# Two indirect scatters of ranks 2 and 3 in flight instead of one, in a mixture-of-experts layer on one core

## The chip, the core and the metric

The kernel runs on one core of a Trainium2 chip, in one launch. The metric is the device time of that launch in microseconds (us). Times of the profile are counted from the start of the span of one profiled execution.

## What is computed

```python
x = layernorm(x + diagonal_ssm_layer(x, Wd, bd, Wi, bi, gamma, beta))
gate = einsum('bsd,ed->bse', x, Wg) + routing_bias
_, top_idx = top_k(gate, 4)
weights = softmax over the 4 chosen, 0 elsewhere
out = swiglu(x, Ws1, Ws2, Ws3)
eo = swiglu of x with each expert's W1, W2, W3
out = out + einsum('ebsd,bse->bsd', eo, weights)
x = layernorm(x + out)
```

There are 2 x 2048 = 4096 tokens of width 256, 8 experts with a hidden size of 682, and 4 experts for each token. The shared expert (Ws1 to Ws3) sees every token. The first layer is a scan along the sequence; it and the routing come before the part that the change touches.

## The kernel before

**Data.** `y_rows` holds the 4096 normed tokens in SBUF as 32 tiles of 128 rows; a row has the token's high and low half-precision parts and its 8 expert weights (264 words of 4 bytes, so a tile is 135 KB). `rows_by_place` (`xs` in the code) is a table in DRAM in which each expert has a contiguous run of places, padded to whole groups of 128 rows. A token stands in it 4 times, once for each of its experts. Its places are sorted, so rank 0 is the place with the token's lowest expert and rank 3 that with its highest.

**Scatter.** On POOL (GpSimd), `scatter(k, overlapped, beside)` (L628 to L641) issues 32 indirect DMAs (L637), one for each tile, that write the tile's rows to their places of rank k. The ranks come one after the other, 0, 1, 2, 3, and after each a `pad_rows` (L623) writes zeros into the padding places of an expert. Two semaphores, `scattered[k][0]` and `scattered[k][1]`, count the even and the odd tiles. For `n < overlapped` tile n waits only for tile n - 2, so two scatters can be in flight; else tile n waits for tile n - 1. Rank 0 has `overlapped` 20, the others have 0.

**Conversion.** The weights of an expert arrive as one DMA of 2.2 MB into the one buffer `stage` (`fetch`, L560), and 12 steps on POOL turn them into a high and a low half-precision part in one of two weight sets in `work` (L563, L564, L570, L573), after which `weight_set_ready` is raised. Expert e uses set e % 2, so its conversion can't start before TensorE (PE) has done with expert e - 2. POOL's program has them in this order:

- the steps of expert 1 between the scatters of rank 1;
- the steps of expert 2 between scatters 1 to 12 of rank 3, with a wait for the end of expert 0 ahead of them (`convert_beside`, L643);
- the fetch of expert 3's weights behind scatter 16 of rank 3;
- after rank 3 the zeros of experts 3 to 7, each of which waits for the one before;
- then a loop over e (L696 to L706). At e = 1 POOL waits for the end of expert 1 and converts expert 3 (`convert(4, 1)`; index 0 is the shared expert's), then fetches the next weights. At e = 2 it waits for the end of expert 2 and converts expert 4, and so on. From e = 4 on each turn also gathers one rank of the experts' results back into `y_sum` (`combine`, L688): 32 indirect DMAs (L682), after the rows of expert e are stored.

**TensorE.** PE runs 9 blocks of 256 tokens of the shared expert, then the experts' blocks by pairs of experts, then the other 7 shared blocks. A block is 66 matmuls up (L942) and 34 down (L965, L970); at the end of an expert there may be a half block of 128 tokens (`xb_half` in the names). Before an expert PE waits for its weight set (L1019). Even experts use the tiles `xb`, odd ones `xb_odd`.

**Loads.** SP loads a block's rows from `rows_by_place` by two transposing DMAs and one small one (`row_weights`), for block b once PE has done the up part of block b - 2. For expert e < 4 it waits first for all of rank e and for the zeros of expert e (L486 to L489).

Between up and down, ACT (L779, L785) and DVE (L1262, L1271) gate the block. L1271 subtracts the high part `g_hi` from `g`, both in SBUF.

Of the kernel before, what the change touches and what calls it, by code (L numbers as in the profile page):

```python
# [59 lines left out]
def build(nc, xT, x_tok, small, wpack, out):  # L60
# [8 lines left out]
    NT = N // P  # L69
# [41 lines left out]
    with ctx:  # L111
# [194 lines left out]
        def low_rank(s):  # L306

            return LOW_ORDER.index(s) + 1
# [9 lines left out]
        def counted(eng, sem_, value):  # L318

            eng.wait_ge(sem_, value)  # L320
            eng.sem_inc(passed, 1)
# [55 lines left out]
        def blocks_until(eng, e):  # L377

            full, half, first, _ = expert_row(eng, e)
            return eng.snap(eng.snap(first + full) + half)  # L380
# [115 lines left out]
        def _(pool):  # L496
# [61 lines left out]
            def fetch(n):  # L558

                pool.dma_start(stage[:, :], wpack[n]).then_inc(weights_loaded, 16)  # L560
# [28 lines left out]
            def convert_step(t, n, w, i):  # L589

                a, m = pieces[i // 2]
                if i == 0:
                    pool.wait_ge(weights_loaded, 16 * n + 16)
                if i % 2 == 0:
                    high_part(t, w, a, m)
                else:
                    t.wait()
                    low_part(t, w, a, m)
                if i == 2 * len(pieces) - 1:
                    t.wait()  # L600
                    pool.sem_inc(weight_set_ready, 1)

            def conversion(n):
                return Tally(pool, convert_steps, 3 * len(pieces) + 1, n - 2)
# [16 lines left out]
            def pad_rows(e):  # L621

                pool.indirect_dma_start(  # L623
                    out=xs, out_offset=bass.IndirectOffsetOnAxis(ap=pad_at[:, e:e + 1], axis=0),
                    in_=zeros[:, :], in_offset=None, bounds_check=NG * P - 1, oob_is_err=False)\
                    .then_inc(pads_written[e], 16)

            def scatter(k, overlapped=0, beside=None):  # L628

                for n in range(NT):  # L630
                    if k == 0 and n % JT == 0:
                        pool.wait_ge(y_low_ready, low_rank(B * (n % (NT // B) // JT) + n // (NT // B)))
                    if n > 1 and (n < overlapped or overlapped and n % 2 == 0):
                        pool.wait_ge(scattered[k][n % 2], 16 * (n // 2))
                    if n > 0 and (n >= overlapped and (n % 2 == 0 or not overlapped)):
                        pool.wait_ge(scattered[k][(n - 1) % 2], 16 * ((n - 1) // 2 + 1))
                    pool.indirect_dma_start(  # L637
                        out=xs, out_offset=bass.IndirectOffsetOnAxis(ap=place[:, k, n:n + 1], axis=0),
                        in_=y_rows[:, n, :], in_offset=None).then_inc(scattered[k][n % 2], 16)
                    if beside:  # L640
                        beside(n)  # L641

            def convert_beside(e, first, fetched):  # L643

                t = conversion(e + 1)

                def step(n):
                    if n == first and e >= 2:
                        counted(pool, down_ready, blocks_until(pool, e - 2) + S1)
                    if 0 <= n - first < 2 * len(pieces):  # L650
                        convert_step(t, e + 1, e % 2, n - first)
                    if n == fetched:
                        fetch(e + 2)
                return step
# [8 lines left out]
            scatter(1, 0, convert_beside(1, 5, 20))  # L663
            pad_rows(1)
            pool.wait_ge(pads_written[1], 16)
            scatter(2)
            pad_rows(2)
            pool.wait_ge(pads_written[2], 16)
            scatter(3, 0, convert_beside(2, 1, 16))
            for e in range(3, E):  # L670
                pool.wait_ge(pads_written[e - 1], 16)
                pad_rows(e)
# [784 lines left out]
```

## Time and profile before

| | us |
|---|---|
| median of 3 runs | 1080.36 (1077.96 to 1081.9) |
| the profiled execution, its time | 1077.3 |
| its span | 1075.5 |
| PE busy (matmuls) | 1007.5 (94%) |
| DVE busy | 581.8 (54%) |
| POOL busy | 533.4 (50%) |
| ACT busy | 501.6 (47%) |
| mean granted TensorE clock | 0.982 of full speed |

Busy shares are means over very different stages; a busy PE is not a PE at its peak, since matmuls are pipelined. POOL's issuing of an indirect DMA counts as busy time, the wait for its landing doesn't. A wait is put down to what the profile infers from semaphore events; "issue" is idle time that it can't put down to anything.

### The profile page before, as it was taken

How to read it: one execution, taken by the hardware profiler on the slowest of the kernel's cores; microseconds unless marked ns; L12 is line 12 of the kernel's file. 1: busy time of each engine (PE TensorE's matmuls, PEld its weight loads, DVE VectorE, ACT ScalarE, POOL GpSimd, SP SyncE). 2: the span in 40 equal slices, each digit the busy share in tenths (PEclk: the TensorE clock that was granted, in tenths of full speed). 3: DMA queues.
4: the chain of work that ended last, by engine and by line, in shares of the span. 5: the costliest groups of instructions: out<-in, count | busy, mean ns of one | idle time of the engine just before them, and what ended most of it. 6: DMA issues, size and time to landing. Idle time of an engine off the chain costs nothing.

```text
span 1075.5 us, 27303 instructions
## 1 busy us (share of the span) xinstructions
PE 1007.5 (94%) x8784; PEld 856.1 (80%) x8785; DVE 581.8 (54%) x1598; ACT 501.6 (47%) x1282; POOL 533.4 (50%) x486
## 2 busy tenths in 40 slices
PE   7997989999999999999889999999999999999985
PEld 3556878778888888888678878978888888888874
DVE  3998896455343435534543435454454444344677
ACT  3675553344454444445334534444444544454454
POOL 3554064376233338623761025075778773676761
PEclk9998999999999999999889999999999999999998
DMA  7846133532633333352234124118763664766674
GB/s 231 225 112 159 21 91 91 153 87 85 168 95 96 86 105 89 94 164 85 56 108 128 49 50 123 44 45 174 113 104 62 110 105 76 119 99 100 86 140 107
DMA packets 167876, 113.84 MB, mean 106 GB/s; under 512 B 113420, under 2 KB 160015, under 8 KB 166672
## 3 DMA queue, kind: packets, MB, share of 16 engines
q0 software_dynamic: 30480, 59.41, 25.7%
q1 hardware_dynamic: 115088, 32.33, 14.9%
q10 hardware_dynamic: 22256, 21.50, 5.8%
q8 instruction: 21, 0.34, 0.2%
q14 instruction: 31, 0.25, 0.1%
HBM read 47.09 MB, written 40.96 MB: 82 GB/s over the span
## 4 chain that ended last, share of the span: by engine, by line
PE 39%; DMA 33%; issue 10%; POOL 9%; DVE 5%; ACT 1%; SPq 1%; ACTq 0%; POOLq 0%; DVEq 0%
PE psA L942 25%; DMA rows_by_place<-y_rows,place 23%; PE psB L965 9%; DMA y_sum<-rows_by_place,place 6%; POOL rows_by_place L637 3%; POOL work L570 2%; PE psA L893 2%; DMA rows_by_place<-zeros,pad_at 2%; PE psB L970 1%; POOL stage L564 1%; POOL work L563 1%; PE psC L924 1%; SPq L475 1%; DMA xb<-rows_by_place 1%; DVE work L1070 1%
## 5 line engine op out<-in xcount | busy, mean ns | idle before, releaser
L1262 DVE SCALAR_TENSOR_TENSOR g<-psA,sil 128x256 f32<-128x256 f32 (+1 forms) x510 | 207.9, 414 | 439.6 <-ACT sil L779 432.5
L779 ACT ACTIVATE sil<-psA 128x256 f32<-128x256 f32 (+1 forms) x510 | 187.2, 373 | 301.7 <-PE psA L942 253.7
L682 POOL DMA_INDIRECT y_sum<-rows_by_place,place x128 | 200.3, 1565 | 105.8 <-DMA y_sum<-rows_by_place,place 78.4
L942 PE MATMUL psA<-xb_odd,work 128*128 128x256 f16 x2112 | 238.4, 274 | 9.0 <-issue 6.0
L637 POOL DMA_INDIRECT rows_by_place<-y_rows,place x128 | 130.3, 1018 | 220.6 <-DMA rows_by_place<-y_rows,place 173.6
L942 PE MATMUL psA<-xb,work 128*128 128x256 f16 x2046 | 231.9, 275 | 7.8 <-DMA row_weights<-rows_by_place 3.8
L942 PEld LDWEIGHTS psA<-xb_odd,work 128*128 128x128 f16 x2112 | 206.9, 98 | 36.7 <-issue 11.4
L785 ACT ACTIVATE g_hi<-g 128x256 f16<-128x256 f32 (+1 forms) x510 | 206.3, 405 | 56.6 <-DVE g L1262 50.9
L965 PE MATMUL psB<-work,g_hi 128*128 128x256 f16 x1320 | 222.1, 273 | 8.1 <-DVE g_lo L1271 7.6
L942 PEld LDWEIGHTS psA<-xb,work 128*128 128x128 f16 x2046 | 201.1, 99 | 34.6 <-issue 9.8
L1271 DVE TENSOR_TENSOR g_lo<-g,g_hi 128x256 f16<-128x256 f32 (+1 forms) x425 | 207.2, 488 | 10.5 <-ACT g_hi L785 6.7
L965 PE MATMUL psB<-work,g_lo 128*128 128x256 f16 x660 | 180.2, 273 | 0.0
L965 PEld LDWEIGHTS psB<-work,g_hi 128*128 128x128 f16 x1320 | 126.3, 98 | 30.1 <-DVE g_lo L1271 14.6
L942 PE MATMUL psA<-xb,wshared 128*128 128x256 f16 x1056 | 120.3, 274 | 3.8 <-DVE g L1262 2.6
L942 PEld LDWEIGHTS psA<-xb,wshared 128*128 128x128 f16 x1056 | 103.4, 98 | 18.0 <-DVE g L1262 3.9
L563 POOL TENSOR_SCALAR work<-stage 128x704 f16<-128x704 f32 (+1 forms) x42 | 37.2, 886 | 122.9 <-PE psB L970 113.3
L965 PEld LDWEIGHTS psB<-work,g_lo 128*128 128x128 f16 x660 | 64.7, 98 | 7.6
L893 PE MATMUL psA<-work,sm 128*128 128x512 f32 x128 | 59.0, 610 | 6.1 <-DMA work<-xT 6.1
L570 POOL TENSOR_TENSOR work<-stage,work 128x704 f16<-128x704 f32 (+2 forms) x42 | 63.1, 1503 | 2.9
L965 PE MATMUL psB<-wshared,g_hi 128*128 128x256 f16 x320 | 54.3, 273 | 8.8 <-DVE g_lo L1271 8.4
L811 ACT ACTIVATE eb<-psB,row_weights_odd 128x256 f32<-128x256 f32 x64 | 26.9, 471 | 70.1 <-PE psB L970 56.6
L811 ACT ACTIVATE eb<-psB,row_weights 128x256 f32<-128x256 f32 x62 | 26.0, 471 | 70.1 <-PE psB L970 53.8
(137 smaller groups left out, 708.2 us busy)
## 6 DMA issues: line engine op xcount, KB each, us to landing
stage<-wpack POOLq DMA_DIRECT2D x9, 2176.0 KB, 9.0
rows_by_place<-eb ACTq DMA_DIRECT2D x63, 256.0 KB
work<-xT SPq DMA_DIRECT2D x8, 512.0 KB, 4.7
work<-half_beta SPq DMA_DIRECT2D x8, 512.0 KB, 5.0
work<-x_tok POOLq DMA_DIRECT2D x8, 512.0 KB, 6.0
rows_by_place<-y_rows,place POOLq DMA_INDIRECT x128, 2.5
y_sum<-rows_by_place,place POOLq DMA_INDIRECT x128, 4.0
out<-y_sum ACTq DMA_DIRECT2D x4, 512.0 KB, 3.7
```

Of the source, the lines that this page charges most:

```text
L563: t.add(pool.tensor_scalar(parts_of(w, a, m)[0], stage[:, a:a + m], WS, 1.0, ALU.mult, ALU.mult))
L570: t.add(pool.tensor_tensor(lo[:, 0:full], stage[:, a:a + full], hi[:, 0:full], ALU.subtract))
L637: pool.indirect_dma_start(out=xs, out_offset=bass.IndirectOffsetOnAxis(ap=place[:, k, n:n + 1], axis=0), in_=y_rows[:, n, :], in_offset=No ...
L682: pool.indirect_dma_start(out=y_sum[:, n, :], out_offset=None, in_=xs, in_offset=bass.IndirectOffsetOnAxis(ap=place[:, k, n:n + 1], axis=0 ...
L779: act.activation(sil[r0:r0 + n, c % SLOTS, 0:T], psA[0:n, c % HVS, 0:T], ACT.Silu, scale=1.0 / (XS * WS)).then_inc(silu_ready, 1)
L785: act.activation(g_hi[0:n, c, 0:T], g32[0:n, c % SLOTS, 0:T], ACT.Copy).then_inc(gated_high_ready, 1)
L811: last = act.activation(eb[:, j, :], psB[:, j, 0:D], ACT.Copy, scale=row_weights[slot][:, j, e:e + 1])
L893: last = pe.matmul(psA[:, q, :], wdi[:, m, w, k, :], xt[b][:, k, :], start=(k == 0), stop=(k == KD - 1))
L942: last = pe.matmul(dst, W[:, ws, k, ci, :], xb[slot][:, KD * xs_ + k, 0:T], start=(k == 0 and n == 0), stop=(k == KD - 1 and n == 2))
L965: pe.matmul(o, a[:, c, j * P:(j + 1) * P], W3[:, ws, c, :], start=(c == 0 and n == 0), stop=False)
L1262: dve.scalar_tensor_tensor(g32[0:n, c % SLOTS, 0:T], src, 1.0 / (XS * WS), sil[r0:r0 + n, c % SLOTS, 0:T], ALU.mult, ALU.mult).then_inc(ga ...
L1271: dve.tensor_tensor(dst, g32[0:n, c % SLOTS, 0:T], g_hi[0:n, c, 0:T], ALU.subtract)\
```

## The change

`scatter` is called with `overlapped` = NT = 32 for ranks 2 and 3 in place of 0. Every tile n > 1 of these ranks then waits for tile n - 2 and not for tile n - 1. Nothing is added or moved on any engine: the instructions and their order are the same on all five, only POOL's waits differ.

```diff
@@ -663,10 +663,10 @@
             scatter(1, 0, convert_beside(1, 5, 20))
             pad_rows(1)
             pool.wait_ge(pads_written[1], 16)
-            scatter(2)
+            scatter(2, NT)
             pad_rows(2)
             pool.wait_ge(pads_written[2], 16)
-            scatter(3, 0, convert_beside(2, 1, 16))
+            scatter(3, NT, convert_beside(2, 1, 16))
             for e in range(3, E):
                 pool.wait_ge(pads_written[e - 1], 16)
                 pad_rows(e)
```

The zeros behind rank 2 (L623) wait for no scatter, before and now, and the first scatter of rank 3 waits for these zeros, not for rank 2's last tile.

## Rows read from the trace of the kernel before

**Rows 1.** Page, part 4: the chain that ended last, by line.

```profile
PE psA L942 25%; DMA rows_by_place<-y_rows,place 23%; PE psB L965 9%; DMA y_sum<-rows_by_place,place 6%; POOL rows_by_place L637 3%; POOL work L570 2%; PE psA L893 2%; DMA rows_by_place<-zeros,pad_at 2%; PE psB L970 1%; POOL stage L564 1%; 
```

**Rows 2.** Timeline of PE: start us, us, engine, line, names, count, idle before.

```profile
524.88 4.14 PE L942 MATMUL psA<-xb_half,work 128*128 128x128 f16 x66 [0.22 <-issue]
...
534.35 0.61 PE L970 MATMUL psB<-work,g_hi 106*128 106x256 f16 x2
540.71 0.61 PE L942 MATMUL psA<-xb_odd,work 128*128 128x256 f16 x2 [5.75 <-issue]
...
554.49 1.04 PE L942 MATMUL psA<-xb_odd,work 128*128 128x256 f16 x8
...
566.82 0.94 PE L942 MATMUL psA<-xb_odd,work 128*128 128x256 f16 x7 [0.46 <-DMA xb_odd<-rows_by_place]
```

**Rows 3.** Windows: us, PE, PEld, DVE, ACT, POOL busy, clock, DMA share, GB/s.

```profile
524.80:540.70 15.90, 7.78 (x83) 5.04 (x83) 6.53 (x12) 4.25 (x15) 14.86 (x15) 0.74 0.17 43
...
345.00:404.00 59.00, 58.94 (x540) 52.76 (x541) 25.02 (x63) 27.37 (x74) 19.67 (x20) 1.00 0.34 96
```

**Rows 4.** Timeline of POOL, from rank 3's scatter 13 to expert 3's conversion.

```profile
444.43 1.24 POOL L637 DMA_INDIRECT rows_by_place<-y_rows,place  x1 [0.82 <-POOL work L573]
...
504.48 1.00 POOL L623 DMA_INDIRECT rows_by_place<-zeros,pad_at  x1 [0.31 <-issue]
...
519.24 0.77 POOL L563 TENSOR_SCALAR work<-stage 128x704 f16<-128x704 f32 x1 [0.93 <-issue]
...
538.78 0.66 POOL L573 TENSOR_TENSOR work<-stage,work 64x256 f16<-64x256 f32 x1
```

**Rows 5.** Line 637 in 308 to 404 us, then in 136 to 170 us.

```profile
L637 POOL DMA_INDIRECT rows_by_place<-y_rows,place x32: 969/969/1212, 308.6 to 400.0; - x32
```

```profile
L637 POOL DMA_INDIRECT rows_by_place<-y_rows,place x20: 965/972/1953, 136.3 to 169.3; - x20
```

**Rows 6.** Timeline of PE: the end of expert 1 and expert 2's first block.

```profile
478.46 0.60 PE L970 MATMUL psB<-work,g_hi 106*128 106x256 f16 x4
480.67 1.59 PE L942 MATMUL psA<-xb,work 128*128 128x256 f16 x13 [1.61 <-DMA row_weights<-rows_by_place]
```

**Rows 7.** Timeline of PE: starts of blocks at other changes of expert.

```profile
641.09 1.29 PE L942 MATMUL psA<-xb,work 128*128 128x256 f16 x7 [2.02 <-issue]
...
653.94 1.04 PE L942 MATMUL psA<-xb,work 128*128 128x256 f16 x8
...
697.63 1.06 PE L942 MATMUL psA<-xb_half,work 128*128 128x128 f16 x16
...
705.71 1.04 PE L942 MATMUL psA<-xb_odd,work 128*128 128x256 f16 x8 [0.88 <-DMA xb_odd<-rows_by_place]
...
717.39 1.16 PE L942 MATMUL psA<-xb_odd,work 128*128 128x256 f16 x9
```

**Rows 8.** Timeline of PE: two blocks of the shared expert during rank 0.

```profile
164.86 1.37 PE L942 MATMUL psA<-xb,wshared 128*128 128x256 f16 x11
...
175.78 1.48 PE L942 MATMUL psA<-xb,wshared 128*128 128x256 f16 x12
```

**Rows 9.** Lines by form, DVE: 345 to 404 us, then 639 to 660 us.

```profile
L1271 DVE TENSOR_TENSOR g_lo<-g,g_hi 128x256 f16<-128x256 f32 x26 | 10.9, 421 | 0.7 <-ACT g_hi L785 0.3
```

```profile
L1271 DVE TENSOR_TENSOR g_lo<-g,g_hi 128x256 f16<-128x256 f32 x7 | 5.9, 837 | 0.0
```

**Rows 10.** Timeline of POOL: first gathers of ranks 2 and 3.

```profile
907.34 1.54 POOL L682 DMA_INDIRECT y_sum<-rows_by_place,place  x1 [14.32 <-DMA rows_by_place<-eb]
...
981.12 1.54 POOL L682 DMA_INDIRECT y_sum<-rows_by_place,place  x1 [3.76 <-DMA rows_by_place<-eb]
```

**Rows 11.** Timeline of SP: one block's load; then PE: that block's start.

```profile
352.92 2.72 SPq L475 DMA_TRANSPOSE xb_odd<-rows_by_place  x2
357.50 0.39 SPq L481 DMA_DIRECT2D row_weights_odd<-rows_by_place  x1
```

```profile
366.91 1.26 PE L942 MATMUL psA<-xb_odd,work 128*128 128x256 f16 x10
```

## The prediction

> **What bounds the kernel now.** I read four views. The chain of waits first: its largest entries are PE's up matmuls and the landings of the scatters of L637, 23% [rows 1]. That share misleads. A chain is followed back through whatever released each step, and for 370 us it runs down POOL's column while PE is busy beside it, all of 58.94 of 59 us between 345 and 404 [rows 3]. A scatter costs the end something only where POOL is late for somebody, so the second view is PE's timeline, to see where PE stood still. There is one large hole: PE ends expert 2 at 534.35 + 0.61 = 534.96 and starts expert 3 at 540.71, idle for 5.75 us with no releaser named [rows 2]. The third view, POOL's timeline, names it: the last instruction of expert 3's conversion starts at 538.78 and takes 0.66, so the weights are ready at 539.4 [rows 4]. The conversion began at 519.24, though PE had done with expert 1, which frees the set, at 478.46 + 0.60 = 479.06 [rows 6]. For 40.2 us POOL had been busy with rank 3 and the zeros. So here POOL's queue, by way of the weight set, is the bound, and nowhere else before the tail. The fourth view, the windows, adds that PE's granted clock is 0.74 around the hole [rows 3], between its two levels of 1.2 and 2.4 GHz, after 1.00 in the steady stretch.
>
> **How early POOL becomes.** Rank 2 issues 32 scatters from 308.6 to 400.0, so 91.4 / 31 = 2.95 us each. Rank 0's first 20, with two in flight, go from 136.3 to 169.3, so 33.0 / 19 = 1.74 us each [rows 5]. I take 1.74; the bounds are 2.95 (a pair gains nothing) and 1.27 (0.97 of issue and the 0.30 that stands between two issues). Rank 2 gains 31 x 1.21 = 37.5 us. In rank 3 the scatters between conversion steps gain nothing: there POOL's arithmetic paces them. From scatter 13 at 444.43 to the first zeros behind rank 3 at 504.48 [rows 4] there are 18 plain intervals, which gain 18 x 1.21 = 21.8. The five zeros keep their waits, 14.8 us from 504.48 to 519.24. Together POOL is 59 us earlier and would reach the turn e = 1 at about 460. There it now waits for expert 1, until 479.1. So of 59 us 40 count, and 19 are slack: a pace up to (91.4 + 58.8 - 40.2) / 49 = 2.24 us would do as well, with 58.8 us from 444.43 to the start of rank 3's last scatter, 1.27 before 504.48.
>
> **What PE gets.** I count from expert 2's first block at 480.67 [rows 6] to expert 3's third at 566.82 [rows 2], 86.15 us before: four full blocks, a half block, two full blocks. Without hole or disturbance a full block takes 175.78 - 164.86 = 10.92 [rows 8]. From a half block to the first block of the next expert in the same pair it is 705.71 - 697.63 = 8.08 [rows 7], against 540.71 - 524.88 = 15.83 now [rows 2]. That makes 6 x 10.92 + 8.08 = 73.60, a gross gain of 12.55 us. It holds the hole, the half block that was slow beside the conversion and at the low clock, and the 2.86 and 1.41 us by which the two blocks at 540.71 and 554.49 exceed 10.92.
>
> **What is given back.** Expert 3's conversion doesn't vanish, it moves to 479.4, beside expert 2's first two blocks. And POOL then fetches expert 4's weights at about 500, so expert 4's conversion starts at once when expert 2 ends, near 532, beside expert 3's first blocks. A conversion slows DVE: L1271 takes 837 ns beside one and 421 ns without [rows 9]. What reaches PE is less, since DVE has idle time in a block. The nearest rows are two conversions that also start at an expert's end: the block at 641.09 takes 12.85, so 1.93 over, and that at 705.71 takes 11.68, so 0.76 over; no later block of either is slow [rows 7]. The first is at a change of pair, as 1 to 2 is; the second is within a pair after a half block, as 2 to 3 is. So I take 1.93 for expert 3's conversion and 0.76 for expert 4's. The upper bound for either is 2.86 + 1.41 = 4.27, the two blocks of expert 3 that now run beside expert 4's conversion [rows 2], which holds clock too; the lower is 0.76. Expert 2's conversion, between the scatters of rank 3, moves 39 us forward from one steady block to another at the same POOL pace: nothing. The fetch behind scatter 16 moves with it: nothing, since the row loads have room (below).
>
> By the Trainium skill's page "SBUF — State Buffer", section "Who interferes with whom", a DVE instruction with two SBUF inputs contends with a GpSimd instruction that reads SBUF, and the loser blocks for a whole instruction. L1271 and all conversion steps are such instructions; were each of L1271's six instructions of a block to wait out a 1.5 us step on PE's path, two blocks would lose 6 x 2 x 1.5 = 18 us, and the sum would be a loss. The trace shows 0.42 us more for each, and 0.76 to 1.93 for a block, so the price of the rows stands.
>
> **The sum.** 12.55 - 1.93 - 0.76 = 9.86 us, bounds 12.55 - 2 x 4.27 = 4.0 and 12.55 - 2 x 0.76 = 11.0. Does it reach the end? Downstream POOL starts each turn when an expert ends or its rows are stored: the gathers of rank 2 waited 14.32 us for expert 6's rows and those of rank 3 waited 3.76 us for expert 7's [rows 10]. These waits are on PE's progress, so POOL follows when PE is earlier, and the last gathers, which end the kernel, start 9.86 us earlier with everything behind them unchanged. The profiled execution would go from 1077.3 to 1067.4. The median stands 3.1 us above the profiled execution; I subtract from the median: 1080.36 - 9.86 = **1070.5 us**.
>
> **Rivals.**
>
> *No overlap in the queue.* The second scatter might only wait behind the first. Pace 2.95, POOL as late as before, 1080.4. Rank 0's pace speaks against it [rows 5], though rank 0 ran beside blocks whose input came from SBUF, not from the table. It decides where POOL gains under about 6 us of its possible 59, so at a pace above 2.83. Chance 0.07.
>
> *The gain is given back.* Both moved conversions cost 4.27 us as in [rows 2]: 12.55 - 8.54 = 4.0, so 1076.4. For it speaks that such a price was measured where expert 4's conversion ran; against it that part of that price was the clock after a hole that will be gone. Chance 0.09.
>
> *Slower: row loads held back.* With two scatters writing to DRAM the loads of expert rows land later. The place is SP's loads for the blocks beside plain scatters: 31 x 1.74 = 54 us of rank 2 and 18 x 1.74 = 31 us of rank 3, about 8 blocks. A load of which the last part is issued at 357.50 + 0.39 and lands some 2.5 us later, taking a scatter's landing for it, is there by 360.4, and its block starts at 366.91 [rows 11]. So 6.5 us are free, and only a load delayed by more than that costs anything. At 8.4 us of delay each block would lose 1.9, 15.2 in all, and the kernel would be slower by 15.2 - 9.86 = 5.3, so 1085.7. A second scatter adds one landing, 2.5 us, so I see no way there. The page "DMA: Bandwidth & Descriptors", section "Queues, rings and completion order", of the Trainium skill says that a semaphore's write lands only after every earlier write of its DMA engine, across its queues; by that rule a load's completion waits for the scatters' writes too, and if loads had no room, 8 blocks x 2.5 us would give 1090.5. The blocks beside rank 0 show no such delay, 10.92 us [rows 8], though their loads read SBUF. Chance 0.03.
>
> *Something downstream keeps part of it*, such as a conversion that falls on a worse moment or gathers that meet other traffic: 1075 to 1079. Chance 0.06.
>
> **How the numbers follow.** The forecast holds 0.75. A measurement of this kernel can tell about 0.5%, 5.4 us, from no change. Of the forecast's range, 4.0 to 11.0 us of gain, nearly all is beyond that. Faster: 0.75, and 0.04 from partial versions of the rivals that still gain over 5.4, so 0.79. Within 0.5%: the first two rivals and the last, 0.17 with what they cede. Slower: 0.04, the third rival and what is unforeseen. The range runs from 1067 (the best case 1069.4, and the 2.4 us by which the lowest of the three runs was under the median) to 1077 (the second rival's 1076.4).
>
> **What would show it.** In the changed profile: L637's 31 intervals of rank 2 take about 54 us; POOL waits for PE's down matmuls ahead of expert 3's conversion, some 19 us that weren't there; that conversion runs from 479.4 to 500; PE has no hole between experts 2 and 3, and 8.1 us stand between the starts of the half block and the next; the clock stays near 1.00 there; L1271 is near 800 ns in 480 to 500, and expert 2's first block takes some 12.8. I am wrong if the hole is there, if blocks beside the plain scatters take more than 10.92, or if the two conversions cost more than 4 us together.

## The result, and the profile after

The changed kernel takes **1113.22 us** (median of 4 runs, 1105.73 to 1117.57), the kernel before 1081.13 beside it (4 runs, 1077.96 to 1083.79): a ratio of 1.0291, interval 1.0225 to 1.0357. I had forecast 1070.5 with 1077 as the upper end. It is slower, where I had given that 4 in 100.

The profiled execution took 1115.4 us, its span is 1113.6, 38.1 more than the 1075.5 before. The page: totals, two rows of the 40 slices, the chain's first lines.

```profile
PE 1023.0 (92%) x8784; PEld 858.2 (77%) x8785; DVE 578.1 (52%) x1598; ACT 502.1 (45%) x1282; POOL 533.3 (48%) x486
...
PE   7997999899975888999999999999999999999985
...
PEclk9998999899995889999999999999999999999998
...
PE 69%; DVE 11%; issue 7%; DMA 5%; ACT 4%; SPq 2%; POOL 1%; ACTq 1%; DVEq 0%; another core or an unknown queue 0%; POOLq 0%
```

DVE, ACT and POOL have the same busy time as before within 4 us. Slices 12 and 13, some 306 to 362 us, have a PE of 7 and 5, and in the second the clock is at 5: that is where rank 2 is scattered. In the chain the scatters have gone from 23% [rows 1] to the 2% that the page gives L637's landings now, and "issue" is at 7%. The windows cut the stretch up:

```profile
core 0: us, PE busy (x) PEld busy (x) DVE busy (x) ACT busy (x) POOL busy (x), PEclk, DMA share, GB/s
312.00:324.00 12.00, 12.00 (x112) 10.75 (x111) 4.22 (x11) 4.62 (x12) 7.15 (x9) 1.00 0.38 113
324.00:337.00 13.00, 5.84 (x32) 3.40 (x31) 2.79 (x7) 2.59 (x7) 9.44 (x10) 0.74 0.34 114
337.00:349.00 12.00, 8.80 (x34) 3.87 (x34) 0.00 (x0) 0.46 (x2) 8.50 (x10) 0.50 0.27 98
349.00:362.00 13.00, 3.78 (x12) 0.94 (x10) 0.26 (x1) 0.77 (x3) 8.36 (x9) 0.50 0.33 116
```

PE goes from 112 matmuls in 12 us to 32 in 13, 34 in 12 and 12 in 13. Its clock falls to 0.50, the lower level of 1.2 GHz, within the 13 us of which it stands still for more than half. The DMA engines are hardly busier than they were: share 0.27 to 0.38 and 98 to 116 GB/s, against 0.34 and 96 in the steady stretch before [rows 3]. Inside the up part of one block, PE, PE's weight loads and POOL run so:

```profile
352.02 0.10 PEld L942 LDWEIGHTS psA<-xb,work 128*128 128x128 f16 x1 [1.31 <-issue]
352.71 0.37 PE L942 MATMUL psA<-xb,work 128*128 128x256 f16 x1 [1.02 <-issue]
352.92 0.97 POOL L637 DMA_INDIRECT rows_by_place<-y_rows,place  x1 [0.63 <-issue]
353.41 0.10 PEld L942 LDWEIGHTS psA<-xb,work 128*128 128x128 f16 x1 [1.29 <-issue]
354.11 0.37 PE L942 MATMUL psA<-xb,work 128*128 128x256 f16 x1 [1.03 <-issue]
354.19 0.97 POOL L637 DMA_INDIRECT rows_by_place<-y_rows,place  x1 [0.30 <-issue]
```

PE issues one instruction in 0.70 us, a weight load and a matmul by turns, though nothing between them waits for a semaphore; "issue" says as much. It isn't PE alone. ACT's next instruction after a block's down part is L811. In the blocks ahead it starts 0.12 us after the last down matmul; here that matmul ends at 336.00 and L811 starts 12.54 us later:

```profile
348.54 0.84 ACT L811 ACTIVATE eb<-psB,row_weights 128x256 f32<-128x256 f32 x2 [15.10 <-remote]
```

SP issues the transposing load of the half block at 332.76, some 9 us after the up part that it waits for; in the kernel before the load of 352.92 [rows 11] comes 0.5 us after its own. DVE isn't shown to be late by itself, its idle time here follows ACT's. I call this **the stall**: from about 324 to 362.6 PE, ACT and SP issue late, but POOL issues a scatter each 1.4 us. It begins 9 us and seven scatters after rank 2's start, and ends where POOL pauses behind rank 2. PE's block starts (a block takes 10.92 undisturbed, [rows 8]), rank 2 and 3 first and then the changes of expert:

```profile
316.39 1.15 PE L942 MATMUL psA<-xb,work 128*128 128x256 f16 x9
...
337.05 0.59 PE L942 MATMUL psA<-xb,work 128*128 128x256 f16 x2 [1.05 <-issue]
...
371.52 1.39 PE L942 MATMUL psA<-xb_half,work 128*128 128x128 f16 x22
...
379.81 1.05 PE L942 MATMUL psA<-xb_odd,work 128*128 128x256 f16 x8 [0.89 <-DMA xb_odd<-rows_by_place]
...
422.66 1.15 PE L942 MATMUL psA<-xb_odd,work 128*128 128x256 f16 x9
...
433.59 1.21 PE L942 MATMUL psA<-xb_odd,work 128*128 128x256 f16 x8
...
453.88 1.15 PE L942 MATMUL psA<-xb_odd,work 128*128 128x256 f16 x9
...
532.09 1.15 PE L942 MATMUL psA<-xb,work 128*128 128x256 f16 x9 [1.61 <-issue]
...
543.09 1.15 PE L942 MATMUL psA<-xb,work 128*128 128x256 f16 x9
...
575.86 1.34 PE L942 MATMUL psA<-xb_half,work 128*128 128x128 f16 x21
...
583.58 1.15 PE L942 MATMUL psA<-xb_odd,work 128*128 128x256 f16 x9 [0.89 <-DMA xb_odd<-rows_by_place]
...
595.26 1.37 PE L942 MATMUL psA<-xb_odd,work 128*128 128x256 f16 x11
...
606.19 1.05 PE L942 MATMUL psA<-xb_odd,work 128*128 128x256 f16 x8
```

The balance against the profiled execution of before:

| where | us | how |
|---|---|---|
| ahead of rank 2, the same code | +1.4 | a block starts at 305.47, before at 304.06 |
| stall in rank 2 | +33.3 | 316.39 to 371.52 is 55.13, less two blocks of 10.92 |
| conversion of expert 2 | +7.3 | 379.81 to 422.66 is 42.85, three blocks and 10.1; before, the blocks there took 12.04 and 12.58, so 2.8 |
| a second stall, beside rank 3's plain scatters | +9.4 | two blocks start 20.29 apart, 433.59 to 453.88 |
| hole ahead of expert 3 gone | -12.0 | 532.09 to 606.19 is 74.10, before 86.15 |
| expert 4's first block | -1.9 | 10.93, before 12.85 [rows 7] |

That is 37.5 of the 38.1 us. POOL's timeline:

```profile
314.88 0.98 POOL L637 DMA_INDIRECT rows_by_place<-y_rows,place  x1 [1.40 <-DMA rows_by_place<-zeros,pad_at]
...
358.37 0.97 POOL L637 DMA_INDIRECT rows_by_place<-y_rows,place  x1 [0.48 <-DMA rows_by_place<-y_rows,place]
...
379.14 0.78 POOL L563 TENSOR_SCALAR work<-stage 128x704 f16<-128x704 f32 x1 [14.56 <-PE psB L970]
...
459.13 1.06 POOL L623 DMA_INDIRECT rows_by_place<-zeros,pad_at  x1 [1.94 <-DMA rows_by_place<-zeros,pad_at]
530.70 0.78 POOL L563 TENSOR_SCALAR work<-stage 128x704 f16<-128x704 f32 x1 [70.51 <-PE psB L970]
```

Rank 2's 31 intervals take 43.5 us, 1.40 each, faster than the 1.74 of my forecast. POOL then waits 14.56 us for the end of expert 0, which the stall had delayed, and 70.51 us for the end of expert 1.

The blocks at expert 2's conversion wait for DVE's L1271. Lines by form, 380 to 414 us, then one instruction of that stretch from DVE's timeline:

```profile
L1271 DVE TENSOR_TENSOR g_lo<-g,g_hi 128x256 f16<-128x256 f32 x10 | 13.8, 1375 | 0.2
```

```profile
401.61 2.56 DVE L1271 TENSOR_TENSOR g_lo<-g,g_hi 128x256 f16<-128x256 f32 x1
```

Before, the same line beside the same conversion (408 to 444 us) took:

```profile
L1271 DVE TENSOR_TENSOR g_lo<-g,g_hi 128x256 f16<-128x256 f32 x15 | 13.2, 879 | 0.2 <-ACT g_hi L785 0.2
```

It would be easy to say that L1271 had run in POOL's waits for landings, which the change removed. But between the steps of this conversion POOL hardly waited before either. Windows over the whole conversion, before and then changed:

```profile
408.40:443.70 35.30, 33.63 (x300) 28.50 (x298) 20.98 (x35) 15.38 (x42) 32.09 (x30) 1.00 0.32 91
```

```profile
379.10:412.90 33.80, 27.64 (x221) 22.24 (x222) 19.59 (x25) 11.26 (x30) 31.41 (x30) 0.90 0.30 85
```

POOL is idle for 3.2 us of 35.3 before and for 2.4 of 33.8 now. In rank3_alone below, which has the change's rank 3, it is idle for 2.4 of 35.0, and L1271 takes 896 ns:

```profile
L1271 DVE TENSOR_TENSOR g_lo<-g,g_hi 128x256 f16<-128x256 f32 x15 | 13.4, 896 | 0.1
```

What differs is which of POOL's instructions each L1271 meets, and what sets that stays open. Part of the 7.3 us is also the clock: it is 0.72 in 400:412, and was 1.00 beside the conversion before.

### The profile page after: what moved, and what is told of

Same layout as the page of the kernel before. It is cut to its first block, busy times and chain, and to the rows that moved or that the text cites. A ratio compares the mean times of both kernels' runs of the same rounds, so it can differ in the third digit from the quotient of the medians.

```text
span 1113.6 us, 27303 instructions
## 1 busy us (share of the span) xinstructions
PE 1023.0 (92%) x8784; PEld 858.2 (77%) x8785; DVE 578.1 (52%) x1598; ACT 502.1 (45%) x1282; POOL 533.3 (48%) x486
## 4 chain that ended last, share of the span: by engine, by line
PE 69%; DVE 11%; issue 7%; DMA 5%; ACT 4%; SPq 2%; POOL 1%; ACTq 1%; DVEq 0%; another core or an unknown queue 0%; POOLq 0%
PE psA L942 46%; PE psB L965 17%; PE psB L970 3%; DVE g_lo L1271 2%; DMA rows_by_place<-y_rows,place 2%; DVE g L1262 2%; PE psA L893 2%; ACT sil L779 1%; DVE stat L1356 1%; PE psC L924 1%; SPq L475 1%; ACT y_sum L853 1%; ACT g_hi L785 1%; POOL rows_by_place L637 1%; DVE work L1070 1%
## 5 line engine op out<-in xcount | busy, mean ns | idle before, releaser
L942 PE MATMUL psA<-xb,work 128*128 128x256 f16 x2046 | 241.3, 278 | 24.8 <-issue 19.2
L942 PE MATMUL psA<-xb_odd,work 128*128 128x256 f16 x2112 | 242.4, 275 | 7.8 <-issue 3.6
L942 PEld LDWEIGHTS psA<-xb,work 128*128 128x128 f16 x2046 | 201.9, 99 | 60.8 <-issue 35.2
L1271 DVE TENSOR_TENSOR g_lo<-g,g_hi 128x256 f16<-128x256 f32 (+1 forms) x425 | 206.5, 486 | 10.3 <-ACT g_hi L785 5.8
L637 POOL DMA_INDIRECT rows_by_place<-y_rows,place x128 | 130.7, 1021 | 149.7 <-DMA rows_by_place<-y_rows,place 94.5
L811 ACT ACTIVATE eb<-psB,row_weights 128x256 f32<-128x256 f32 x62 | 26.0, 471 | 80.9 <-PE psB L970 46.5
L811 ACT ACTIVATE eb<-psB,row_weights_odd 128x256 f32<-128x256 f32 x64 | 26.9, 471 | 77.8 <-PE psB L970 55.4
```

The lines of the kernel that those rows point to most:

```text
L637: pool.indirect_dma_start(out=xs, out_offset=bass.IndirectOffsetOnAxis(ap=place[:, k, n:n + 1], axis=0), in_=y_rows[:, n, :], in_offset=No ...
L811: last = act.activation(eb[:, j, :], psB[:, j, 0:D], ACT.Copy, scale=row_weights[slot][:, j, e:e + 1])
L942: last = pe.matmul(dst, W[:, ws, k, ci, :], xb[slot][:, KD * xs_ + k, 0:T], start=(k == 0 and n == 0), stop=(k == KD - 1 and n == 2))
L1271: dve.tensor_tensor(dst, g32[0:n, c % SLOTS, 0:T], g_hi[0:n, c, 0:T], ALU.subtract)\
```

## The experiments

The recorded expectations call the theories by letters. **P**: the pace, a dense row of scatters starves the engines' issue. **L**: the rival of the prediction, row loads land late. **F**: two scatters in flight are harmful as such. **B**: both ranks must be changed for the stall to appear. **C**: it depends on the chip that the runs fall on. The kernels of one group ran on one chip and share its runs of the kernel before; the ratio is to these, with a 95% interval. The diffs of the two spaced kernels, of narrow_rows and of drained_every_8 are against the changed kernel, the others against the kernel before; declarations are left out.

**First chip** (before: 1074.03). In this order: rank2_alone, rank3_alone, pairs_both, and rank0_all_32, which gives all 32 scatters of rank 0 what its first 20 have.

```diff
-            scatter(2)
+            scatter(2, NT)
```

```diff
-            scatter(3, 0, convert_beside(2, 1, 16))
+            scatter(3, NT, convert_beside(2, 1, 16))
```

```diff
-            scatter(2)
+            scatter(2, 1)
-            scatter(3, 0, convert_beside(2, 1, 16))
+            scatter(3, 1, convert_beside(2, 1, 16))
```

```diff
-            scatter(0, 20)
+            scatter(0, NT)
```

With `overlapped` = 1 an odd tile waits for nothing and an even one for both before it: two scatters 1.28 us apart, then a pause until both have landed.

> Theory P (pace): scatters that follow each other every 1.4 us, kept up for some 6 of them, starve every engine of instructions, and the loss comes only from the two plain stretches. Rank 2 alone then has the first stall of 33 us (blocks of 20.7 and 34.5 us where 10.92 is normal), no stall in rank 3, and no hole between experts 2 and 3 (12 us back): about 33 - 12 = 21 us over the kernel before, some 1102 us. Rival L (loads): the loss is row loads that land late because two scatters write to DRAM; it would give the same total here, but PE would wait for a DMA between blocks and not inside one.

> Theory P: rank 3 alone has the second stall (9 us), the slower blocks beside the conversion (7 us more than before, since POOL leaves DVE no gap) and saves the hole (12 us) as POOL is some 22 us earlier: 1081 + 9 + 7 - 12 = about 1085 us. If the stall in rank 3 needed what rank 2 left behind, it is about 1076.

> Ranks 2 and 3 scatter in pairs: an even tile waits for both before it, an odd one for nothing. Theory P: the pace is about 2.25 us a scatter (4.5 a pair, as in the last 12 of rank 0), two are in flight half of the time, POOL is some 34 us earlier, no stall, no hole: 12 us under the kernel before, less what conversions cost, 1069 to 1073 us. Rival F (two in flight as such, whatever the pace): stalls stay, at least half as long as in the change, so 1085 or more.

> Only rank 0 is changed: all its 32 tiles two in flight, where the last 12 went in pairs; PE runs the shared expert's blocks then, which load from SBUF and are no loop. Theory P alone: at a pace of 1.4 us the blocks between 170 and 190 us stall too, and the kernel gets slower by 5 to 20 us. Theory P with a place (the stall needs the experts' loop, or traffic to and from the table in DRAM): blocks stay at 10.92 us, expert 0 starts up to 10 us earlier or not at all earlier, and the time is 1072 to 1081 us.

| | us (range, runs) | ratio |
|---|---|---|
| rank2_alone | 1065.21 (1063.73 to 1070.01, 9) | 0.9931 [0.9904, 0.9959] |
| rank3_alone | 1069.80 | 0.9966 [0.9937, 0.9995] |
| pairs_both | 1068.74 | 0.9946 [0.9916, 0.9977] |
| rank0_all_32 | 1068.58 | 0.9948 [0.9918, 0.9978] |

All four end the hole: expert 3 starts 7.6 to 7.7 us after the half block, rank0_all_32 included. In rank0_all_32 expert 3's conversion starts at 508.21, only 11 us earlier than before (519.24, [rows 4]): that is enough to end the hole, as the slack in the prediction had it. No stall in any of them, not even in rank2_alone, whose rank 2 is the change's. Its pace (L637 in rank 2) and its windows:

```profile
L637 POOL DMA_INDIRECT rows_by_place<-y_rows,place x32: 967/970/1225, 312.3 to 357.8; - x32
```

```profile
324.00:337.00 13.00, 13.00 (x124) 11.65 (x123) 4.94 (x13) 5.21 (x15) 8.83 (x9) 1.00 0.47 140
337.00:349.00 12.00, 10.09 (x118) 8.24 (x116) 4.10 (x15) 5.33 (x18) 7.77 (x8) 1.00 0.55 163
```

45.5 / 31 = 1.47 us each, and PE issues 124 and 118 matmuls in the windows where the change issued 32 and 34. P as it stood expected 1102 us of rank2_alone and 1085 of rank3_alone, and both are faster than the kernel before. Either rank 3 must be dense too for a stall in rank 2 (B), or this chip differs from the result's (C).

**Second chip** (before: 1075.81). The change itself, and rank 2 dense with rank 3 in pairs:

```diff
-            scatter(2)
+            scatter(2, NT)
-            scatter(3, 0, convert_beside(2, 1, 16))
+            scatter(3, 1, convert_beside(2, 1, 16))
```

> The changed kernel itself, unedited, beside the kernel before, since rank 2 alone showed no stall though its program up to rank 3 is the change's. Theory C (the stall is of the chip or its surroundings, not of the change's instructions): no stall here, no hole between experts 2 and 3, about 1064 to 1068 us where before is 1074. Theory B (both ranks are needed, for instance since rank 3 shifts what meets what): the stalls are back in all runs, 1105 to 1117 us. If some of its runs are near 1066 and others near 1110, it is a state that a run falls into.

> Rank 2 two in flight throughout, rank 3 in pairs. Theory B: the stall of rank 2 (33 us) would be back if any overlap in rank 3 brings it, about 1095; if it needs full overlap there, about 1065. Theory C: 1064 to 1068 us, as rank 2 alone, since POOL's lead from rank 2 already fills the hole and more lead only waits for the end of expert 1.

change_again: 1115.17 (1113.03 to 1118.52, 6 runs), ratio 1.0345 [1.0303, 1.0387], with a block of 46.50 us in rank 2 and one of 20.74 in rank 3. rank2_full_rank3_pairs: 1099.79 (4 runs), 1.0211 [1.0156, 1.0265], a block of 41.43 us in rank 2, none over 10.92 beside rank 3's plain scatters. So each dense rank makes its own stall, and pairs in rank 3 make none, on one chip.

This chip shows a beginning of it in code that the change doesn't touch. Beside rank 0's scatters the block at about 154 us takes 11.22 in the kernel before; on this chip it takes 16.48 in change_again and 17.39 in rank2_alone_third (below), but 11.22 to 12.36 in the chip's four other profiles. Windows of rank2_alone_third, then of the kernel before:

```profile
157.00:164.00 7.00, 5.46 (x38) 2.99 (x37) 1.18 (x4) 0.87 (x3) 4.67 (x5) 0.97 0.25 87
```

```profile
157.00:164.00 7.00, 6.87 (x64) 5.90 (x63) 5.86 (x14) 4.67 (x12) 4.01 (x4) 1.00 0.38 110
```

From scatter 8 to scatter 15 of rank 0 (counted from 0) the mean interval is 1.42 and 1.44 us in the two profiles with the long block, and 1.58 to 1.82 in the four without. The faster pace can be the cause of the long block or come from it.

**Third chip** (before: 1076.31). The change, rank2_alone and pairs_both once more, and the change with a gap, still two in flight: behind each plain scatter of ranks 2 and 3 POOL clears an unused tile.

```diff
+                    if k >= 2 and (k == 2 or n > 12):
+                        turns_spaced[0] += 1
+                        pool.wait_ge(spaced, turns_spaced[0] - 1)
+                        pool.memset(spacer[:, :], 0.0).then_inc(spaced, 1)
```

> The unedited change once more, as the yardstick for the three other kernels of this call on this one chip: the first four kernels ran on one chip and the two after them on another. Theory C (the stall depends on the chip): near 1115 us on one that stalls, near 1066 on one that doesn't. Theory B (both ranks are needed): 1115 us in any case.

> Rank 2 alone, unedited, on the chip of the yardstick. Theory C: if the yardstick is at 1115, this one has the 33 to 40 us stall of rank 2 and is at 1098 to 1106, and not at 1065 as it was on the other chip. Theory B: 1065 us although the yardstick is at 1115.

> The change, with a memset of a tile that nobody reads (about 0.4 us on POOL) behind each scatter of rank 2 and behind the plain ones of rank 3; still two in flight. The pace goes from 1.4 to about 1.75 us, that of rank 0's first 20. Theory P (pace decides): no stall or little of it, 1066 to 1080 us also where the yardstick is at 1115. Rival F (two in flight as such): the stall stays and gets longer, as the stretch does, 1115 us or more.

> Ranks 2 and 3 in pairs, unedited, on the chip of the yardstick. Theory P: the mean pace of 2.25 us lets whatever fills drain between pairs, 1066 to 1073 us. Rival F: part of the stall, 1085 us or more, where the yardstick has it.

| | us | ratio |
|---|---|---|
| change_third | 1068.77 (1065.25 to 1071.73, 9) | 0.9932 [0.9900, 0.9963] |
| rank2_alone_again | 1066.71 | 0.9912 [0.9881, 0.9944] |
| spaced_two_in_flight | 1073.01 | 0.9962 [0.9927, 0.9998] |
| pairs_both_again | 1068.81 | 0.9944 [0.9910, 0.9978] |

Here the change itself is **faster** by 7.5 us, 0.7% with an interval clear of 1, and has no stall. Pace and windows of change_third:

```profile
L637 POOL DMA_INDIRECT rows_by_place<-y_rows,place x32: 967/970/1157, 311.4 to 357.6; - x32
```

```profile
312.00:324.00 12.00, 12.00 (x113) 10.73 (x111) 5.83 (x16) 6.14 (x17) 8.11 (x9) 1.00 0.45 135
324.00:337.00 13.00, 13.00 (x122) 11.63 (x120) 5.53 (x14) 5.55 (x15) 9.02 (x9) 1.00 0.43 134
```

Is it a slower pace that saves it? Over rank 2 it is 46.2 / 31 = 1.49, against 1.38 to 1.43 where the stall is. But the first eight intervals, which lie ahead of the stall, take 1.45 us each here and 1.43 to 1.51 in the six stalling profiles of a dense rank 2. The paces part only later, when the stalled kernels have fewer other transfers. So at an equal pace it is there in one group and not in the other, and C gains ground. But for expert 2's conversion (below) the stall-free profile is as forecast: the hole is gone, and expert 2's first block to expert 3's third is 74.1 us.

**Fourth chip** (before: 1077.06). The change again, pairs and spacing again, and the change with a quarter of the bytes in the scatters: ranks 2 and 3 write 66 of the 264 words of a row into a table of their own.

```diff
-            spare = K * N
+            spare = 0
...
-                        out=xs, out_offset=bass.IndirectOffsetOnAxis(ap=place[:, k, n:n + 1], axis=0),
-                        in_=y_rows[:, n, :], in_offset=None).then_inc(scattered[k][n % 2], 16)
+                        out=xs if k < 2 else narrow,
+                        out_offset=bass.IndirectOffsetOnAxis(ap=place[:, k, n:n + 1], axis=0),
+                        in_=y_rows[:, n, :] if k < 2 else y_rows[:, n, 0:66], in_offset=None).then_inc(scattered[k][n % 2], 16)
```

narrow_rows leaves out the rows of ranks 2 and 3: their places keep zeros, which are written to the whole table at the start. Its total is therefore no measure; its stall is.

> Yardstick for this call: the unedited change. It was at 1113 and 1115 us on two occasions and at 1069 on a third. Theory C (the stall depends on the chip): one or the other here, all its runs alike, and the three kernels beside it are read by it.

> Ranks 2 and 3 write only the first 66 of each row's 264 words, to a table of their own in DRAM that nobody reads; the whole row table is zeroed at the start instead. Left out: those tokens' rows for experts of rank 2 and 3. Same number of row writes and same pace, a quarter of the bytes. If bytes written to DRAM, or writes to the table that others read, make the stall: none here even where the yardstick has it, 1070 to 1085 us (the zeroing may cost some). If the number of row writes per us makes it: the stall is there, 1110 to 1125 us where the yardstick is at 1115.

> Pairs in ranks 2 and 3, unedited, where the yardstick stalls if it does. Theory P: mean pace 2.25 us, no stall, 1066 to 1073 us on any chip. Rival F: part of the stall, 1085 us or more where the yardstick has it.

> The change with a memset behind each plain scatter (pace 1.75 us or more), unedited. Theory P: no stall where the yardstick has it, 1070 to 1080 us. Rival F: the stall is there, 1100 us or more.

| | us | ratio | longest blocks in rank 2 |
|---|---|---|---|
| change_fourth | 1106.05 (1098.17 and 1113.93) | 1.0249 [1.0119, 1.0379] | 22.01 and 28.64 |
| narrow_rows | 1167.55 (2 runs) | 1.0819 [1.0771, 1.0868] | 48.92 |
| pairs_both_third | 1075.05 (9 runs) | 0.9965 [0.9928, 1.0002] | 12.59 |
| spaced_again | 1072.44 (6 runs) | 0.9961 [0.9912, 1.0011] | 10.92 |

The stall is back with the change. The windows of change_fourth, then of spaced_again, with rank 2's row of the latter:

```profile
324.00:337.00 13.00, 7.17 (x48) 4.07 (x45) 3.45 (x9) 2.75 (x8) 9.14 (x10) 0.89 0.31 108
```

```profile
L641 POOL DMA_INDIRECT rows_by_place<-y_rows,place x32: 977/980/1219, 311.3 to 362.8; - x32
```

```profile
324.00:337.00 13.00, 13.00 (x122) 11.63 (x120) 6.42 (x17) 6.28 (x17) 11.37 (x16) 1.00 0.38 120
```

51.5 / 31 = 1.66 us each in spaced_again, many of them 1.55, still two in flight, and PE issues 122 matmuls where the change issued 48. F falls: it isn't two in flight. Nor is it how busy POOL is, 11.37 of 13 us here and 9.14 in the change.

A little may stay. In the half block beside rank 2, PE loses 1.2 to 1.4 us in the three profiles of pairs or spacing on this chip and the second (9.47, 9.68 and 9.52 us, against 8.28 and 8.29 in pairs on the other two). In pairs_both_third and rank2_pairs the clock falls behind it, and the next block takes 12.59. The kernel before wasn't profiled on these chips, so that may be the chip's and not the scatters'. Of narrow_rows, rank 2's row and windows:

```profile
L638 POOL DMA_INDIRECT narrow<-y_rows,place x32: 965/969/1210, 354.5 to 395.6; - x32
```

```profile
362.00:374.00 12.00, 7.20 (x40) 3.29 (x38) 0.42 (x1) 1.22 (x3) 8.61 (x10) 0.78 0.15 47
374.00:386.00 12.00, 5.89 (x21) 1.88 (x20) 1.51 (x4) 1.37 (x4) 9.26 (x10) 0.50 0.09 26
```

Scatters 41.1 / 31 = 1.33 us apart with a quarter of the bytes: the stall is as hard, at 26 GB/s and a DMA share of 0.09. Neither the bytes nor the DMA engines' time carry it, nor do writes to the table that the loads read. What is left is the number of scatters, or of their rows, in a time: 128 rows each in either case.

**Second chip again** (before: 1076.30). The change; rank 2 alone, to settle B; the change with a halt at every eighth scatter, where POOL waits for both before it (intervals of 3.2 to 4.1 us in place of 1.4); pairs in rank 2 alone, `scatter(2, 1)`, as a version that might beat both.

```diff
-                    if n > 0 and (n >= overlapped and (n % 2 == 0 or not overlapped)):
+                    if n > 0 and (n >= overlapped and (n % 2 == 0 or not overlapped) or k >= 2 and n % 8 == 0):
```

> Yardstick for this call, the unedited change: near 1066 to 1070 us or near 1100 to 1116, as on the chips so far, and all its runs alike.

> Rank 2 alone, unedited. It was at 1065 and 1067 us on two chips, on the second of which the change ran at 1069. Theory C: with the yardstick at 1100 or more it has the stall of rank 2 too, 1090 to 1106 us; with the yardstick near 1068 it is at 1065 to 1068. Theory B (needs rank 3 too) falls if it stalls.

> The change, but every 8th tile of ranks 2 and 3 waits for both before it, so a run of 8 scatters at 1.4 us is followed by a pause of 1.3 us; mean pace 1.55 us. Where the yardstick stalls: if a mean rate decides and its limit lies above 1.55 us, the stall is there with most of its length, 1090 us or more; if the limit lies under 1.55, or a pause empties what has filled, there is none, 1066 to 1075 us.

> Only rank 2 in pairs, rank 3 as before. POOL's lead is 31 x 0.7 = 22 us: expert 3's conversion ends near 517, before expert 2 does, so the hole is gone (12 us back, less 2 to 3 for the moved conversions), and rank 3's conversion keeps its old gaps. 1066 to 1071 us on any chip, stalling or not, as fast as pairs in both ranks or better.

| | us | ratio |
|---|---|---|
| change_fifth | 1118.69 (2 runs) | 1.0406 [1.0353, 1.0459] |
| rank2_alone_third | 1099.71 (1098.74 to 1103.28, 3) | 1.0237 [1.0193, 1.0282] |
| drained_every_8 | 1097.87 (3 runs) | 1.0208 [1.0163, 1.0253] |
| rank2_pairs | 1075.08 (1070.93 to 1083.84, 10) | 0.9999 [0.9961, 1.0037] |

B falls: the kernel that gained 0.7% and 0.9% on two chips loses 2.4% on this one, with the same code and rank 3 untouched. Its windows, to set against those of rank2_alone above:

```profile
324.00:337.00 13.00, 7.67 (x43) 3.88 (x41) 2.80 (x8) 2.75 (x8) 9.53 (x10) 0.87 0.26 94
```

The halts spread the stall and don't end it. Windows of drained_every_8:

```profile
322.00:334.00 12.00, 8.71 (x72) 6.65 (x71) 1.74 (x5) 2.04 (x6) 7.77 (x8) 1.00 0.44 135
334.00:346.00 12.00, 10.51 (x77) 8.27 (x78) 3.36 (x9) 4.07 (x11) 7.86 (x8) 0.86 0.27 90
```

72 and 77 matmuls in 12 us, between the 112 of a free stretch and the change's 32 to 34; its blocks there take 13.27, 16.79 and 15.37 us, and the half block 14.86. Its mean pace is 1.62, near spaced_again's 1.66, but in bursts with a median interval of 1.36. So on this evidence the interval within a run of eight counts, not the mean; the two kernels ran on different chips, both of which stall, so this last step is weaker than the others.

rank2_pairs has neither stall nor hole, expert 3 starts 7.69 us after the half block, and yet it gains nothing. Its profiled execution (1079.47) is 4.4 us over its median. Against the profile of before it gives back 2.9 us at the half block and the block behind it, 3.8 beside expert 2's conversion (12.45, 13.61 and 13.25 us, 6.6 over three times 10.92, against 2.8), and 6.9 ahead of rank 2, where the program is the same (blocks up to 15.97). From expert 2's first block to expert 3's third it gains 11.0. That leaves some 4 us of gain behind the start of rank 2 in that profile; the interval, 0.9961 to 1.0037, neither shows nor excludes as much.

**Best version.** None beats the kernel before everywhere. rank2_alone is the best where there is no stall (0.9931, 0.9912) and costs 2.4% where there is one. Two in flight in pairs, or spaced to 1.55 us, gave 0.9946, 0.9944, 0.9965 and 0.9962, 0.9961: about half a per cent at best, and no loss on the three and two chips that they ran on, of which one stalls. On that one both intervals reach 1, so no gain is shown there. pairs_both is the one I would keep; it didn't run on the second chip, where rank2_pairs gained nothing.

## Why the prediction was wrong

**The path and the hole: right.** POOL's queue was the bound at expert 3 through the weight set. From expert 2's first block to expert 3's third I forecast 12.55 us less, and 9.86 after the price of two conversions; it is 12.05 after that price. The half block stands 7.72 us ahead of the next (forecast 8.08).

**Two conversions: over-priced.** I had 1.93 and 0.76 us. Expert 2's first block takes 543.09 - 532.09 = 11.00, so 0.08; expert 3's takes 11.68, so 0.76. The first number came from a block at a change of pair [rows 7], which takes 10.93 in place of 12.85 now, though a conversion still runs beside it. Those 1.93 us were the clock, not the conversion. The window over the block's start in the trace of before:

```profile
641.00:645.00 4.00, 3.92 (x21) 2.90 (x22) 0.43 (x1) 0.38 (x1) 3.92 (x4) 0.57 0.14 33
```

In the changed kernel the clock is 1.00 there.

**Expert 2's conversion, "from one steady block to another at the same POOL pace: nothing": wrong.** It cost 7.3 us in the change and 5.7 in change_third (blocks of 11.42, 11.48, 17.84, 11.40, against 2.8 over before). The premise held, POOL's pace there is the same (12 steps and the scatters between them in 33.6 us, before 35.2), and the conclusion didn't: between 8 and 11 us over undisturbed blocks in all six profiles with both ranks dense, 4.4 in rank3_alone. The price hangs on how L1271 and POOL's instructions fall together, and I had taken one such case for all. The rule of the Trainium skill's page "SBUF — State Buffer", section "Who interferes with whom", that the loser blocks for a whole instruction, fits 2.56 us for an instruction of 0.42 only if it loses more than once: POOL's longest step there takes 1.65. I had weighed that rule for the moved conversions and not for this one.

**The pace: off, and harmful where it was thought a bonus.** I took rank 0's 1.74 us [rows 5] and set 1.27 as the lower bound with the remark that a faster pace would only be slack. It is 1.40. Something in rank 0 costs 0.34 us more for each, and I read its 1.74 as the price of two in flight; what it is no run tells.

**The failed step is what dense scatters do to their neighbours, which the sum put at nothing and the third rival at one landing, 2.5 us a block, inside 6.5 us of room.** The runs show 33.3 us in rank 2 and 9.4 in rank 3. The rival had the right sign and place, the blocks beside plain scatters, and the wrong mechanism: loads that land late. I dismissed it, among other reasons, since "The blocks beside rank 0 show no such delay, 10.92 us [rows 8]". That row was taken at 1.74 us a scatter, and on the second chip a block beside rank 0 does stretch, to 17.39. spaced_again agrees with the row, 10.92 at 1.55 to 1.66 us. The change left the range that any row of before had shown, and a bound worked out from neighbours (6.5 us of room, a landing of 2.5) said nothing of what happened outside it. The stall is no late load: PE stands inside a block whose rows and weights are there, and ACT and SP issue late as well. By the completion rule of the Trainium skill's page "DMA: Bandwidth & Descriptors", section "Queues, rings and completion order", I had priced the worst case at 1090.5; the result is 23 us above it, and narrow_rows shows that the bytes written don't carry it.

**On a chip without the stall the gain is in the range**: 1068.77 against a before of 1076.31 is 7.5 us less, inside my 4.0 to 11.0. Part of that is luck. The span is 7.3 us shorter: 12.05 and expert 4's 1.9 gained, 5.7 lost at expert 2's conversion, 1 us elsewhere; I had 2.7 for the moved conversions and nothing for expert 2's.

**What stays open.** Which shared resource the scatters take from the instruction supply isn't shown. Instruction fetches by DMA are a candidate. Of the packets of the two queues that the page calls "instruction", none starts between 274.0 and 377.2 us in the changed kernel, so they don't show it; the kernel before has four from 342.5 to 358.5, in blocks that the changed kernel reaches only behind the stall. Why two chips (three, if the result's was another) have the stall and two haven't is open as well, and four chips are few: only the second was used twice, so for the others chip and occasion aren't told apart. The limit lies between the 1.43 to 1.51 us ahead of the stalls and the 1.59 of spaced_again's first eight intervals; nothing between was tried.

## What to carry to other kernels

A queue that is made faster must be priced for what its speed does to everybody else, not only for the waits that it ends: if the new pace lies beyond any that the trace shows, the neighbours' "no delay" is no evidence, and the range must say so. Keep dense rows of indirect DMAs from GpSimd apart (pairs, a short instruction between). Don't take the price of one stretch in which POOL and DVE work side by side for that of another: the same conversion cost 2.8 us and 10.1. Look at the granted clock of a row before its excess is put down to a neighbour. And measure such a change on more than one chip: the same code was 0.7% faster on one and 4% slower on another.

## What the runs showed of the hardware

- With indirect scatters of 128 rows 1.4 us apart, PE, its weight loads, ACT and SP issue slowly after some 9 us: one PE instruction in 0.70 us, at a DMA share near 0.3. A quarter of the bytes changes nothing (share 0.09). At an even 1.55 us or more (fourth chip), or in pairs (second and fourth), chips that stall run their full blocks in 10.92 us, with 1.2 to 1.4 us lost in a half block. The Trainium skill's page "SBUF — State Buffer", section "Who interferes with whom", says that DMA never contends with a compute engine and that PE and ACT never wait on anyone. That section is on ports, and no run here bears on these; read as a statement on what DMAs can do to an engine's progress it doesn't hold here.
- It went with the chip: present on two of four (both times on the second chip, and on the fourth), absent on the first and third at the same pace.
- The granted clock followed PE down to 0.50 (1.2 GHz) during the stall and was 1.00 in 368:374, but 0.72 again in 400:412 and in 440:452, where PE stood still for 4.3 of 12 and 3.0 of 12 us. Before, 0.57 in 641:645 made a block of 10.92 us one of 12.85.
- L1271, 0.42 us alone, took up to 2.65 us beside expert 2's conversion (change_third), and on average 0.88 in the kernel before (POOL idle for 3.2 us of that stretch), 0.90 in rank3_alone (2.4) and 1.38 in the changed kernel (2.4). What decides between these was not shown.
